# A new order of the calls on four engines in one period of a software-pipelined attention kernel

## The chip, the core and the metric

The kernel runs on 1 core of one Trainium2 chip. The metric is the device time of one execution in microseconds. Before the change three runs gave 4885.24 (median), 4884.3 and 4894.25 us.

## What is computed

A block of three parts on 8 x 256 tokens of width 256, in float32, each with a residual: half an FFN, an attention-like layer, half the same FFN. The layer has 16 heads. For each head it makes a query, four keys and four values a token by a projection, a causal convolution of width 4 and silu; the query and keys are normalised; a decay comes from a softplus of a low-rank projection. Then the state is carried over the tokens with a delta rule:

```python
M = tril(einsum(kg * exp(Gt - Gs), beta * kg), -1)        # chunk x 4 keys, square
u = solve_triangular(I + M, vg - einsum(kg * exp(G), S))
o = SCALE * (einsum(qg * exp(G), S) + einsum(attn, u))
S = exp(Glast)[..., None] * S + einsum(beta * kg * exp(Glast - G), u)
...
o = o * rsqrt(mean(o * o) + eps) * onorm_w * sigmoid(gate);  out = o @ Wo.T
```

## The kernel before

`build` cuts the 2048 tokens in NT = 4 tiles of 512 (two sequences), which with 16 heads makes NS = 64 sets. In a set there are 16 units of 32 tokens with 4 keys each, so that a unit is a matrix of 128 x 128; for each of the two sequences (hb = 0, 1) the eight units c = 0 to 7 follow one another through the state S.

The first FFN runs by itself. Then the sets run as a software pipeline: in period p (`for p in range(-1, NS + 3)`, L1045, L1430, L1805, L2010) every engine works on four sets, p to p - 3. Each engine has one list of calls written out by hand, one of the functions `delta_tensor` (L823), `delta_scalar` (L1168), `delta_vector` (L1541) and `delta_gpsimd` (L1940). An engine works through its list in order; between engines every call waits for counters that other calls raise (`nth`, `every`), so the order of a list decides what stands behind what, and never what is computed. Set p + 1 and p: `project_k`, `conv_k` (three taps on DVE after `tap_k` on ACT), `silu_k`, `decay`, `softplus`, `add_up` (a prefix sum), `factors` (exponentials). Set p - 1: `project_v`, `conv_v`, `silu_v`, `products` (for each quarter q of the set five levels l, whose scaled operands X come from `levels` on DVE and `level` on GpSimd), `evacuate` (Pd) and `keep` (E, At) of the results, `take`, `norm` (three small steps, the second after `length(0)` of ACT), `weigh`. Set p - 2: `begin` and `rows` on GpSimd, which invert the diagonal 32 x 32 blocks in 62 steps; when the last is done `unfold` and `turn` on DVE lay the result out, ACT's `place` (four copies) and `shift` put it in Ztf and Zc, and `first` to `fourth`, on PE and ACT by turns, build the inverse of the unit from it. Sets p - 2 and p - 3: the chunk steps `rhs`, `solve` and `update` of both sequences: PE `rhs`, DVE `rhs` (Rs), PE `solve`, ACT `solve` (Us), PE `update`, DVE `update` (S). At the end of set p - 3: ACT `out_square`, PE `mean_square`, ACT `out_root`, DVE `gated`, PE and DVE `output`.

The PSUM results (k, v, decay, norm, turned kdec and V, mean square, output, gate) share two banks in turn. `turns` (L692) takes a list in the order in which PE issues them (`bank_use`, L702) and gives every use its bank and the counter that says that the use before it on this bank is emptied; `acc_use` (L712) does so for three accumulators of the convolutions.

ACT's functions need one of two tables, with exp and ln or with silu and tanh. `e.preload_act_table_set` (L1444, L1471, L1510) names a point where the first is loaded ahead of its use; other switches are put in ahead of the function that needs them (they show under the helper line L1182).

In the last periods `spare(s, j)` calls (all four lists have them at points of the same name) do pieces of the second FFN (`DRAIN`, L23): a piece of gate and up matmuls, or of the down matmul. In all other periods they are empty.

## Time and profile before

| | |
|---|---|
| runs | 4885.24 us median (4884.3 to 4894.25) |
| span of the profiled execution | 4882.9 us |
| its own time beside the span | not given apart; the median of the runs is 2.3 us above the span |
| mean granted clock of TensorE | 0.979 |
| first FFN | the first 243 us or so |
| periods that follow one another in full | about 500 to 4510 us |
| last two periods and second FFN | 4510 us to the end |

The page gives the busy time of each engine as a share of the span; matmuls overlap, so a busy PE is not one at its peak. The trace behind it gives each instruction with its start, its length, and, where the engine stood idle before it, how long and which engine's work ended the wait. Two things matter in reading: a helper line stands for many calls (L835 for most matmuls, L1553 and L1556 for most of DVE, L1181 and L1182 for ACT), so operations are told by their tiles; and an instruction of DVE or ACT is longer than the distance to the next, because the two overlap.

### The profile page before, as it was taken

To read this page: it belongs to the slowest core of one execution; us is meant where nothing else is said; L and a number is where in the kernel's file an instruction comes from. 1 tells how busy PE (TensorE), PEld (TensorE's weight loads), DVE (VectorE), ACT (ScalarE), POOL (GpSimd) and SP (SyncE) were. 2 spreads that over 40 slices of the span, in tenths; PEclk is the share of its full clock that TensorE was granted. 3 is DMA by queue.
4 is the path that set the end of the run, shared out by engine and by line. 5 is a ranking of instruction groups with operands and counts; after the bars stand their busy time and mean duration, and the time that the engine had idled before them with its cause. 6 is when DMAs were issued, how large, how long until landed. Compare 5 with 4: busy or idle time off the path is not lost.

```text
span 4882.9 us, 151877 instructions
## 1 busy us (share of the span) xinstructions
PE 4493.2 (92%) x63200; PEld 3127.3 (64%) x63200; DVE 4052.7 (83%) x7262; ACT 3391.0 (69%) x6708; POOL 3362.7 (69%) x5828
## 2 busy tenths in 40 slices
...
GB/s 88 88 29 25 26 26 26 15 25 26 34 32 16 28 26 26 26 14 26 35 32 28 15 26 26 26 25 14 30 30 26 26 14 26 26 26 9 37 9 22
DMA packets 49727, 135.48 MB, mean 28 GB/s; under 512 B 7056, under 2 KB 28176, under 8 KB 48400
## 3 DMA queue, kind: packets, MB, share of 16 engines
...
## 4 chain that ended last, share of the span: by engine, by line
PE 58%; DVE 26%; ACT 9%; issue 6%; POOL 1%; DMA 0%; DVEq 0%; SPq 0%; ACTq 0%
PE bank L835 49%; DVE acc L1556 9%; PE bank L302 7%; DVE X L1553 6%; PE bank L906 2%; DVE Rs L1556 2%; DVE Pd L1661 2%; ACT o L1182 1%; DVE sp_t L1553 1%; DVE Zc L1740 1%; ACT Us L1181 1%; DVE o L1556 1%; ACT acc L1181 1%; ACT L1471 1%; ACT Ztf L1181 1%
## 5 line engine op out<-in xcount | busy, mean ns | idle before, releaser
L1556 DVE SCALAR_TENSOR_TENSOR acc<-bank,vc,acc 128x510 f32<-128x510 f32 (+2 forms) x1728 | 1270.9, 739 | 145.5 <-ACT acc L1181 120.0
L2006 POOL TENSOR_TENSOR LZ<-LZ,LT 128x120 f32<-128x120 f32 (+26 forms) x1984 | 979.5, 494 | 155.5
L2003 POOL TENSOR_TENSOR LT<-LA,LZ 128x120 f32<-128x120 f32 (+26 forms) x1984 | 877.8, 442 | 145.8
L1553 DVE TENSOR_TENSOR X<-KQ,Fl 128x640 f32<-128x640 f32 x1024 | 966.6, 960 | 0.9 <-ACT Fl L1182 0.9
L1976 POOL COPY X<-KQ 128x640 f32<-128x640 f32 x256 | 255.9, 1000 | 807.5 <-ACT F L1182 278.3
L835 PEld LDWEIGHTS bank<-X 128*32 128x32 f32 x32768 | 524.0, 112 | 301.0 <-issue 210.8
L1181 ACT ACTIVATE Us<-bank 128x128 f32<-128x128 f32 x1024 | 280.7, 277 | 627.8 <-PE bank L835 617.3
L835 PE MATMUL bank<-X 128*32 128x60 f32 (+1 forms) x32768 | 650.3, 205 | 64.4 <-issue 32.6
L835 PE MATMUL bank<-xnTm,WK 128*128 128x512 f32 x1280 | 660.8, 642 | 41.5 <-DVE acc L1556 35.8
L1951 POOL TENSOR_TENSOR kdec<-KQ,Fe 128x256 f32<-128x256 f32 x512 | 461.0, 921 | 152.3 <-PE bank L906 152.3
L835 PE MATMUL bank<-Rs,Ztf 128*128 128x128 f32 x2048 | 460.7, 312 | 68.1 <-DVE Rs L1556 48.0
L835 PE MATMUL bank<-xnTm,WV 128*128 128x512 f32 x1024 | 497.3, 608 | 12.8 <-ACT sg L1182 6.7
L1556 DVE SCALAR_TENSOR_TENSOR Rs<-V,knT,bank 128x128 f32<-128x128 f32 x896 | 308.1, 344 | 206.0 <-PE bank L835 194.2
L1181 ACT ACTIVATE acc<-bank,vc 128x512 f32<-128x512 f32 x576 | 393.7, 684 | 79.6 <-PE bank L835 77.2
L835 PEld LDWEIGHTS bank<-Rs,Ztf 128*128 128x128 f32 x2048 | 314.5, 191 | 193.5 <-DVE Rs L1556 113.9
L835 PE MATMUL bank<-Us,kdT 128*128 128x128 f32 x1792 | 399.5, 306 | 41.7 <-ACT Us L1181 23.6
L1951 POOL TENSOR_TENSOR kexp<-KQ,Fe 128x256 f32<-128x256 f32 x512 | 424.1, 855 | 0.0
L835 PEld LDWEIGHTS bank<-xnTm,WK 128*128 128x128 f32 x1280 | 230.2, 200 | 275.3 <-issue 172.1
L835 PE MATMUL bank<-S,kexp 128*128 128x128 f32 x1792 | 388.6, 299 | 3.2 <-ACT S L1181 2.6
L835 PE MATMUL bank<-qn,S 128*128 128x32 f32 x1792 | 349.2, 277 | 0.0
L835 PEld LDWEIGHTS bank<-S,kexp 128*128 128x128 f32 x1792 | 282.8, 192 | 80.1 <-issue 34.8
L835 PEld LDWEIGHTS bank<-Us,kdT 128*128 128x128 f32 x1792 | 272.6, 192 | 93.9 <-ACT Us L1181 78.7
...
## 6 DMA issues: line engine op xcount, KB each, us to landing
...
```

Source lines behind the costliest of these rows:

```text
L302: return e.matmul(o, l, r, start=start, stop=stop, skip_group_check=True)
L835: return e.matmul(o, l, r, start=start, stop=stop, skip_group_check=True)
L906: ins = e.transpose(o[:, P * c:P * c + P], kdec[:, c, :], ident)
L1181: return e.activation(o, i, f, scale=scale)
L1182: return e.activation(o, i, f, bias=bias, scale=scale)
L1553: return e.tensor_tensor(o, a, b, op)
L1556: return e.scalar_tensor_tensor(out=o, in0=a, scalar=sc, in1=b, op0=op0, op1=op1)
L1661: return e.copy_predicated(o, mk, d.rearrange("p n (a c) -> p n a c", c=c))
L1951: return e.tensor_tensor(o.rearrange("p u (g i t) -> p (u g) i t", g=4, i=R), kq[:, g0:g0 + 8, 0:R, :], f.unsqueeze(2).broadcast_to([P, 8, ...
L1976: e.tensor_copy(X0[:, :, 0:40], kk.rearrange("p g i t -> p g (i t)")).then_inc(g_copy, 1)
L2003: e.tensor_tensor(tmp, LA[:, j + 1:32, 8 * (j % R) + j // R].unsqueeze(2).broadcast_to([P, rr, cc]), LZ[:, j, 0:cc].unsqueeze(1).broadcast ...
L2006: e.tensor_tensor(LZ[:, j + 1:32, 0:cc], LZ[:, j + 1:32, 0:cc], tmp, SUB).then_inc(g_row, 1)
```

## The change

The four lists are laid out anew, and `bank_use` follows PE's new order (norm and the fourth turned V change places). No call is added or taken away, but the boundaries of a period are cut at other points, so that some calls stand in a period's head in one list and at the tail of the previous one in the other (`products(p, 0, 1)` for `products(p - 1, 0, 1)`, `length(p - 1, 1)` for `length(p - 2, 1)`). The first of the three `preload_act_table_set` calls now stands at the head of ACT's period. The diff, with the indentation taken off:

```diff
@@ -705,8 +705,8 @@
-("vturn", 2, 2, a_vt, 4, 2), ("turn", 0, 1, a_kdT, 4, 0), ("norm", 0, 0, v_max, 1, 0),
-("vturn", 3, 2, a_vt, 4, 3), ("turn", 1, 1, a_kdT, 4, 1), ("k", 0, -1, v_ck, 15, 2),
+("vturn", 2, 2, a_vt, 4, 2), ("turn", 0, 1, a_kdT, 4, 0), ("vturn", 3, 2, a_vt, 4, 3),
+("norm", 0, 0, v_max, 1, 0), ("turn", 1, 1, a_kdT, 4, 1), ("k", 0, -1, v_ck, 15, 2),
 ("k", 1, -1, v_ck, 15, 5), ("turn", 2, 1, a_kdT, 4, 2),
...
@@ -1043,59 +1043,58 @@
 for p in range(-1, NS + 3):
-rhs(p - 3, 0, 3)
-products(p - 1, 0, 1)
+update(p - 3, 1, 2)
+spare(p - 3, 7)
 solve(p - 3, 0, 3)
-update(p - 3, 1, 2)
-spare(p - 3, 8)
 turn(p - 2, 3)
 update(p - 3, 0, 3)
+spare(p - 3, 8)
 rhs(p - 3, 1, 3)
+rhs(p - 3, 0, 4)
 project_k(p, 2)
-rhs(p - 3, 0, 4)
 solve(p - 3, 1, 3)
+solve(p - 3, 0, 4)
+products(p - 1, 0, 2)
+update(p - 3, 1, 3)
...
 update(p - 3, 1, 5)
-spare(p - 3, 17)
-products(p - 1, 0, 4)
 solve(p - 3, 0, 6)
 rhs(p - 3, 1, 6)
+products(p - 1, 0, 4)
+spare(p - 3, 17)
 solve(p - 3, 1, 6)
-spare(p - 3, 19)
 update(p - 3, 0, 6)
 update(p - 3, 1, 6)
+spare(p - 3, 19)
+rhs(p - 3, 0, 7)
+rhs(p - 3, 1, 7)
+project_v(p - 1, 1)
 spare(p - 3, 20)
-rhs(p - 3, 0, 7)
-project_v(p - 1, 1)
 solve(p - 3, 0, 7)
-rhs(p - 3, 1, 7)
+solve(p - 3, 1, 7)
 project_k(p, 3)
-solve(p - 3, 1, 7)
+update(p - 3, 0, 7)
 spare(p - 3, 22)
-update(p - 3, 0, 7)
 update(p - 3, 1, 7)
+mean_square(p - 3)
 spare(p - 3, 23)
-mean_square(p - 3)
 project_k(p, 4)
...
@@ -1107,63 +1106,64 @@
 gate(p - 1)
 project_v(p - 1, 2)
+project_v(p - 1, 3)
 products(p - 1, 2, 0)
 products(p - 1, 2, 1)
-project_v(p - 1, 3)
+spare(p - 2, 30)
 first(p - 2, 0)
-spare(p - 2, 30)
 products(p - 1, 2, 2)
+spare(p - 2, 31)
 second(p - 2, 0)
-spare(p - 2, 31)
 products(p - 1, 2, 3)
+products(p - 1, 2, 4)
 turn_v(p - 2, 1)
-products(p - 1, 2, 4)
 third(p - 2, 0)
 spare(p - 2, 32)
 turn_v(p - 2, 2)
 turn(p - 1, 0)
 fourth(p - 2, 0)
 spare(p - 2, 33)
+turn_v(p - 2, 3)
 total(p)
-turn_v(p - 2, 3)
+first(p - 2, 1)
 products(p - 1, 3, 0)
-first(p - 2, 1)
-spare(p - 2, 34)
 products(p - 1, 3, 1)
-turn(p - 1, 1)
-second(p - 2, 1)
-spare(p - 2, 35)
 products(p - 1, 3, 2)
 products(p - 1, 3, 3)
+spare(p - 2, 34)
+second(p - 2, 1)
+products(p - 1, 3, 4)
+spare(p - 2, 35)
+turn(p - 1, 1)
 solve(p - 2, 0, 0)
-products(p - 1, 3, 4)
 project_k(p + 1, 0)
+update(p - 2, 0, 0)
 third(p - 2, 1)
+rhs(p - 2, 0, 1)
+fourth(p - 2, 1)
 spare(p - 2, 36)
-update(p - 2, 0, 0)
 project_k(p + 1, 1)
-fourth(p - 2, 1)
+solve(p - 2, 1, 0)
+solve(p - 2, 0, 1)
 spare(p - 2, 37)
-rhs(p - 2, 0, 1)
-solve(p - 2, 1, 0)
+update(p - 2, 1, 0)
+update(p - 2, 0, 1)
 spare(p - 2, 1)
-solve(p - 2, 0, 1)
-update(p - 2, 1, 0)
+rhs(p - 2, 1, 1)
 spare(p - 2, 2)
-update(p - 2, 0, 1)
-rhs(p - 2, 1, 1)
+rhs(p - 2, 0, 2)
 turn(p - 1, 2)
-rhs(p - 2, 0, 2)
 solve(p - 2, 1, 1)
+products(p, 0, 0)
+solve(p - 2, 0, 2)
+update(p - 2, 1, 1)
 spare(p - 2, 4)
-update(p - 2, 1, 1)
+products(p, 0, 1)
 spare(p - 2, 5)
-solve(p - 2, 0, 2)
 rhs(p - 2, 1, 2)
 update(p - 2, 0, 2)
-products(p, 0, 0)
 solve(p - 2, 1, 2)
-spare(p - 2, 7)
+rhs(p - 2, 0, 3)
...
@@ -1428,115 +1428,115 @@
 for p in range(-1, NS + 3):
-solve(p - 3, 1, 2)
-factors(p - 1, 3)
+e.preload_act_table_set("natural_log_exp_and_others")
 spare(p - 3, 7)
 solve(p - 3, 0, 3)
-turned(p - 2, 2)
+spare(p - 3, 8)
 silu_k(p, 0)
-silu_k(p, 1)
+turned(p - 2, 3)
+solve(p - 3, 1, 3)
+solve(p - 3, 0, 4)
 tap_k(p, 2)
-spare(p - 3, 8)
-solve(p - 3, 1, 3)
-turned(p - 2, 3)
 spare(p - 3, 10)
-solve(p - 3, 0, 4)
-e.preload_act_table_set("natural_log_exp_and_others")
-length(p - 2, 1)
+spare(p - 3, 11)
 factors(p - 1, 4)
-spare(p - 3, 11)
...
-decay(p, 1)
+spare(p - 3, 19)
+silu_k(p, 1)
+spare(p - 3, 20)
+tap_v(p - 1, 1)
+solve(p - 3, 0, 7)
+solve(p - 3, 1, 7)
 silu_k(p, 2)
-tap_v(p - 1, 1)
-spare(p - 3, 19)
-spare(p - 3, 20)
-solve(p - 3, 0, 7)
 silu_v(p - 1, 0)
-solve(p - 3, 1, 7)
 tap_k(p, 3)
+spare(p - 3, 22)
 out_square(p - 3)
 e.preload_act_table_set("natural_log_exp_and_others")
-decay(p, 2)
-spare(p - 3, 22)
 spare(p - 3, 23)
 out_root(p - 3, 0)
 out_root(p - 3, 1)
+decay(p, 1)
 keep(p - 1, 0)
 tap_k(p, 4)
 keep(p - 1, 1)
+decay(p, 2)
 silu_k(p, 3)
+gate_out(p - 1)
+shift(p - 2)
+turned_v(p - 2, 0)
 silu_v(p - 1, 1)
-gate_out(p - 1)
-turned_v(p - 2, 0)
-shift(p - 2)
 place(p - 2, 0)
+tap_v(p - 1, 2)
 place(p - 2, 1)
 place(p - 2, 2)
 place(p - 2, 3)
-tap_v(p - 1, 2)
+spare(p - 2, 30)
 silu_k(p, 4)
 tap_v(p - 1, 3)
+spare(p - 2, 31)
 first(p - 2, 0)
 square(p)
-spare(p - 2, 30)
 second(p - 2, 0)
-spare(p - 2, 31)
+keep(p - 1, 2)
 turned_v(p - 2, 1)
 third(p - 2, 0)
 spare(p - 2, 32)
 turned_v(p - 2, 2)
 turned(p - 1, 0)
+spare(p - 2, 33)
 fourth(p - 2, 0)
-keep(p - 1, 2)
-spare(p - 2, 33)
+silu_v(p - 1, 2)
+silu_v(p - 1, 3)
 turned_v(p - 2, 3)
-silu_v(p - 1, 2)
+rhs(p - 2, 0, 0)
 first(p - 2, 1)
-rhs(p - 2, 0, 0)
-silu_v(p - 1, 3)
 e.preload_act_table_set("natural_log_exp_and_others")
+spare(p - 2, 34)
+rhs(p - 2, 1, 0)
+spare(p - 2, 35)
 root(p, 0)
-spare(p - 2, 34)
-turned(p - 1, 1)
+solve(p - 2, 0, 0)
 second(p - 2, 1)
 root(p, 1)
-spare(p - 2, 35)
-solve(p - 2, 0, 0)
-rhs(p - 2, 1, 0)
 tap_k(p + 1, 0)
+update(p - 2, 0, 0)
+turned(p - 1, 1)
 third(p - 2, 1)
 factors(p, 0)
+spare(p - 2, 36)
 length(p - 1, 0)
-spare(p - 2, 36)
-update(p - 2, 0, 0)
 keep(p - 1, 3)
 fourth(p - 2, 1)
+factors(p, 1)
+solve(p - 2, 1, 0)
 spare(p - 2, 37)
-solve(p - 2, 1, 0)
+solve(p - 2, 0, 1)
+length(p - 1, 1)
+tap_k(p + 1, 1)
+update(p - 2, 1, 0)
+factors(p, 2)
 spare(p - 2, 1)
-solve(p - 2, 0, 1)
-update(p - 2, 1, 0)
-factors(p, 1)
-tap_k(p + 1, 1)
 spare(p - 2, 2)
 solve(p - 2, 1, 1)
-factors(p, 2)
+turned(p - 1, 2)
+factors(p, 3)
 spare(p - 2, 4)
+solve(p - 2, 0, 2)
 spare(p - 2, 5)
-solve(p - 2, 0, 2)
+solve(p - 2, 1, 2)
...
@@ -1803,139 +1803,139 @@
 for p in range(-1, NS + 3):
+spare(p - 3, 5)
+rhs(p - 3, 1, 2)
+update(p - 3, 0, 2)
 conv_k(p, 1, 1)
-spare(p - 3, 7)
 rhs(p - 3, 0, 3)
 conv_k(p, 1, 0)
+spare(p - 3, 7)
 levels(p - 1, 0, 2)
 update(p - 3, 1, 2)
+update(p - 3, 0, 3)
+spare(p - 3, 8)
 distance(p - 1, 4)
...
+spare(p - 3, 22)
 conv_k(p, 3, 2)
 conv_k(p, 3, 1)
-evacuate(p - 1, 0, 1)
+spare(p - 3, 23)
 conv_k(p, 3, 0)
-evacuate(p - 1, 0, 2)
 evacuate(p - 1, 0, 3)
 query(p - 1)
-spare(p - 3, 22)
-spare(p - 3, 23)
+lengths(p - 2)
 gated(p - 3, 0)
 gated(p - 3, 1)
 conv_k(p, 4, 2)
 conv_k(p, 4, 1)
+evacuate(p - 1, 1, 0)
 conv_k(p, 4, 0)
-evacuate(p - 1, 1, 0)
-output(p - 3, 0)
 evacuate(p - 1, 1, 1)
 evacuate(p - 1, 1, 2)
+output(p - 3, 0)
+evacuate(p - 1, 1, 3)
 output(p - 3, 1)
-evacuate(p - 1, 1, 3)
 unfold(p - 2, 0)
 unfold(p - 2, 1)
+levels(p - 1, 2, 1)
 turn(p - 2)
-levels(p - 1, 2, 1)
+softplus(p)
 levels(p - 1, 2, 2)
 levels(p - 1, 2, 3)
 levels(p - 1, 2, 4)
 conv_v(p - 1, 2, 2)
+spare(p - 2, 30)
 conv_v(p - 1, 2, 1)
+spare(p - 2, 31)
 conv_v(p - 1, 2, 0)
 conv_v(p - 1, 3, 2)
 conv_v(p - 1, 3, 1)
+evacuate(p - 1, 2, 0)
 conv_v(p - 1, 3, 0)
-evacuate(p - 1, 2, 0)
+levels(p - 1, 3, 1)
+spare(p - 2, 32)
+add_up(p)
 evacuate(p - 1, 2, 1)
+spare(p - 2, 33)
 evacuate(p - 1, 2, 2)
-levels(p - 1, 3, 1)
-softplus(p)
 levels(p - 1, 3, 2)
 evacuate(p - 1, 2, 3)
+levels(p - 1, 3, 3)
+levels(p - 1, 3, 4)
+spare(p - 2, 34)
 clamp(p)
-lengths(p - 2)
-levels(p - 1, 3, 3)
-add_up(p)
-levels(p - 1, 3, 4)
-distance(p, 1)
+spare(p - 2, 35)
 evacuate(p - 1, 3, 0)
 evacuate(p - 1, 3, 1)
 evacuate(p - 1, 3, 2)
+distance(p, 1)
 evacuate(p - 1, 3, 3)
 take(p - 1)
 scale(p)
+spare(p - 2, 36)
 norm(p - 1, 0)
 distance(p, 2)
+rhs(p - 2, 0, 1)
+norm(p - 1, 1)
 conv_k(p + 1, 0, 2)
-norm(p - 1, 1)
+norm(p - 1, 2)
 conv_k(p + 1, 0, 1)
-norm(p - 1, 2)
-spare(p - 2, 30)
-spare(p - 2, 31)
-spare(p - 2, 32)
-spare(p - 2, 33)
-spare(p - 2, 34)
-spare(p - 2, 35)
-spare(p - 2, 36)
 spare(p - 2, 37)
-rhs(p - 2, 0, 1)
 weigh(p - 1)
 conv_k(p + 1, 0, 0)
 spare(p - 2, 1)
+update(p - 2, 0, 1)
 spare(p - 2, 2)
-update(p - 2, 0, 1)
 rhs(p - 2, 1, 1)
 distance(p, 3)
 rhs(p - 2, 0, 2)
+conv_k(p + 1, 1, 2)
 levels(p, 0, 1)
 spare(p - 2, 4)
 update(p - 2, 1, 1)
-conv_k(p + 1, 1, 2)
-spare(p - 2, 5)
-rhs(p - 2, 1, 2)
-update(p - 2, 0, 2)
...
@@ -2023,11 +2023,11 @@
 spread(p - 1, 0, 0)
 spread(p - 1, 0, 1)
+spread(p - 1, 1, 0)
 spread(p - 1, 1, 1)
-spread(p - 1, 1, 0)
 spread(p - 1, 2, 1)
+spread(p - 1, 3, 1)
 spread(p - 1, 2, 0)
-spread(p - 1, 3, 1)
 level(p, 0)
```

## Rows read from the trace of the kernel before

**Rows 1.** The page, part 1: busy us, share of the span, instructions, by engine.
```profile
PE 4493.2 (92%) x63200; PEld 3127.3 (64%) x63200; DVE 4052.7 (83%) x7262; ACT 3391.0 (69%) x6708; POOL 3362.7 (69%) x5828
```
**Rows 2.** Windows view of four stretches: length, busy us by engine, clock, DMA share, GB/s.
```profile
436.39:4440.10 4003.71, 3745.78 (x57113) 2646.93 (x57112) 3620.05 (x6431) 3001.44 (x6019) 3105.64 (x5369) 0.99 0.07 25
2399.62:2468.30 68.68, 64.46 (x969) 45.11 (x969) 61.45 (x110) 50.85 (x102) 53.71 (x93) 0.98 0.10 35
3619.58:3686.45 66.87, 62.82 (x969) 44.62 (x969) 61.20 (x110) 50.82 (x103) 52.53 (x92) 1.00 0.09 31
...
2460.70:2464.20 3.50, 3.42 (x8) 1.05 (x12) 2.55 (x6) 2.16 (x5) 2.99 (x7) 0.57 0.00 0
```
**Rows 3.** Timeline of DVE, first and last of 60 turns: start us, length us.
```profile
436.39 0.71 DVE L1748 STREAM_TRANSPOSE Ztc<-Zc 128x512 f32<-128x512 f32 x1
...
4440.10 0.71 DVE L1748 STREAM_TRANSPOSE Ztc<-Zc 128x512 f32<-128x512 f32 x1
```
**Rows 4.** Timeline of PE, one period from its gate, and one wait in the tail.
```profile
3619.58 1.02 PE L835 MATMUL bank<-fgm,WV 128*128 128x512 f32 x2
...
3626.05 0.69 PE L835 MATMUL bank<-Zc,E 32*32 32x32 f32 x32
...
3627.28 0.21 PE L835 MATMUL bank<-Ys,Ztf 32*32 32x32 f32 x1 [0.15 <-ACT Ys L1181]
...
3634.66 0.52 PE L835 MATMUL bank<-X 128*32 128x60 f32 x24 [0.35 <-DVE Pd L1661]
...
3646.64 0.71 PE L835 MATMUL bank<-Rs,Ztf 128*128 128x128 f32 x4 [0.26 <-ACT Ztf L1181]
...
3670.58 0.49 PE L835 MATMUL bank<-Rs,Ztf 128*128 128x128 f32 x2 [0.44 <-DVE Rs L1556]
...
3678.51 1.10 PE L835 MATMUL bank<-o,cs 128*128 128x512 f32 x2 [0.78 <-ACT o L1182]
3680.05 1.98 PE L835 MATMUL bank<-xnTm,WK 128*128 128x512 f32 x4 [0.44 <-DVE acc L1556]
...
4691.71 1.06 PE L835 MATMUL bank<-Zc,E 32*32 32x32 f32 x32 [4.62 <-ACT Ztf L1181]
```
**Rows 5.** Timeline of ACT, opening of this period: place (four) and tap_v(2).
```profile
3622.55 2.59 ACT L1181 ACTIVATE Ztf<-Ztc 32x512 f32<-32x512 f32 x4
3625.17 0.69 ACT L1181 ACTIVATE acc<-bank,vc 128x512 f32<-128x512 f32 x1
```
**Rows 6.** Timeline of ACT, end of this period: out_square, decay(2), out_root(0).
```profile
3677.77 0.60 ACT L1182 ACTIVATE o<-bank 128x512 f32<-128x512 f32 x1
...
3679.68 0.72 ACT L1182 ACTIVATE rn<-rn,cs 128x512 f32<-128x512 f32 x1
3680.31 0.67 ACT L1182 ACTIVATE o<-bank,cs 128x512 f32<-128x512 f32 x1
```
**Rows 7.** Timeline of DVE, this period: norm(2), conv_k(4), the next unfold.
```profile
3646.05 0.25 DVE L1553 TENSOR_TENSOR Cn<-Cn,LB 128x32 f32<-128x32 f32 x1
...
3683.13 2.30 DVE L1556 SCALAR_TENSOR_TENSOR acc<-bank,vc,acc 128x510 f32<-128x510 f32 x3
...
3687.45 1.18 DVE L1740 STREAM_TRANSPOSE Zc<-LZ 128x256 f32<-128x256 f32 x2
```
**Rows 8.** Timeline of POOL, this period: begin and the last step of rows.
```profile
3646.36 0.53 POOL L1985 MEMSET LZ<- 128x512 f32 x1
...
3685.89 0.22 POOL L2006 TENSOR_TENSOR LZ<-LZ,LT 128x16 f32<-128x16 f32 x1
```
**Rows 9.** Timeline of ACT: a load in this period; two loads in the tail.
```profile
3655.72 1.28 ACT L1182 ACT_TABLE_LOAD   x1
3657.02 1.15 ACT L1182 ACTIVATE KQ<-acc 128x512 f32<-128x512 f32 x2
...
4793.80 1.28 ACT L1471 ACT_TABLE_LOAD   x1
...
4796.52 1.28 ACT L1510 ACT_TABLE_LOAD   x1
```

More of the change, by code:

```diff
@@ L1056, in delta_tensor @@
                 solve(p - 3, 1, 3)
+                solve(p - 3, 0, 4)
+                products(p - 1, 0, 2)
+                update(p - 3, 1, 3)
                 spare(p - 3, 10)
-                solve(p - 3, 0, 4)
-                update(p - 3, 1, 3)
+                rhs(p - 3, 1, 4)
+                update(p - 3, 0, 4)
                 spare(p - 3, 11)
-                update(p - 3, 0, 4)
-                rhs(p - 3, 1, 4)
                 project_v(p - 1, 0)
-                products(p - 1, 0, 2)
```

55 lines of the change are left out of this document (27 added, 28 removed).

## The prediction

> **What bounds it now.** The page's engine shares come first: TensorE (PE) 92% busy, VectorE (DVE) 83%, ScalarE (ACT) 69% [rows 1]. No engine is full, so order can matter. Next the stages: the stretch in which all sets overlap, 4003.71 us, is 59 periods between the first and the last turn of DVE [rows 2, 3], so 67.86 us for one. The period from 3619.58 takes 66.87 at full granted clock, the one from 2399.62 takes 68.68 with 3.5 us at 0.57 in it [rows 2]: an undisturbed period is 66.87, and about 1.0 of the mean is disturbance, partly the clock. I work on the undisturbed one, and count its times from its gate matmul (3619.58 is 0). Inside it the timeline of PE shows short waits [rows 4]: 0.15 for ACT's Ys, 0.35 for DVE's last Pd, 0.26 for ACT's Ztf, 0.44 for DVE's Rs in the chunk steps, then 0.78 for ACT's square and 0.44 for DVE's conv_k(3,0), which frees the bank of project_k(4). Adding small ones it is some 4 us in 66.87; an order can only win some of these. The path changes engine every few us, so I walked the new lists by hand: each operation begins when its engine has issued what stands ahead of it and its producer is done, with durations and start-to-start distances of the same operations in the old period. A wait on a short operation costs little, so distances matter: an isolated conv tap is 0.74 long, but the next begins 0.66 after it.
>
> **Opening: costs 0.63.** The four place copies take 2.59 on ACT and stand at 2.97 to 5.56 [rows 5]. In the new list decay(2) (0.65) stands ahead of the load and silu_k(3), silu_v(1) (0.6) stands behind turned_v(0), and tap_v(2) (0.69, [rows 5]) inside the four. The gate waits 0.27 longer, since evacuate(1,0) goes ahead of the last tap of conv_k(4) on DVE. By these the first place starts at 3.98 and the last ends at 7.19 in place of 5.56. PE reaches first(0) at 6.74 and stands 0.50 there (it began at 6.47 before, [rows 4]); with tap_v(3) and the Ys copy (ending 8.65) behind it, second(0) starts at 8.69, not 7.70, +0.99. Then cover comes back. conv_v(3,0) ends 0.8 later (softplus is ahead of it), in time for turn_v(2). add_up (1.2) goes ahead of evacuate(2,3), but PE no longer stands at products(3,0) for it: it does turn_v(3), total and first(1) first, so the 0.35 [rows 4] goes. PE has products(3,0) still to issue at 16.33; before it had issued it and first(1) at 16.26. That is 0.63 late with the 0.56 of products(3,0) counted.
>
> **Middle: gives back 0.46.** With turn(1) behind products(3,4) the wait of 0.20 for levels(3,4) goes, and project_k(0) ends at 22.07 against 21.81. third(1) on ACT now has tap_k(0), update(0,0) and turned(1) ahead of it (0.58 + 0.18 + 0.6), so PE waits 0.6 at fourth(1); project_k(1) behind it covers the wait of solve(1,0) for Ztf (0.26, [rows 4]). update(1,0) starts at 28.37 against 27.92; update(1,2), after conv_k(1,0..2) and levels(0,1) at DVE, at 35.00 against 35.16, with solve(0,3) (0.32) still to do: 0.17 late.
>
> **Chunk steps: win 0.56.** Each step is solve to update 0.86, update to S 0.51, S to rhs about 0.4, rhs to Rs 0.5, Rs to solve 0.4, and twelve of them must be threaded between the big matmuls. From 35 to 49 the two orders come out alike (update(1,5) begins 0.15 late). Then products(0,4) stands between rhs(1,6) and solve(1,6) and covers the wait of 0.44 for Rs [rows 4]; rhs(1,7) is ahead of project_v(1), and both solves ahead of project_k(3), whose 1.7 covers the Us copies. project_k(3) ends at 56.60 with solve(1,7) issued, against 56.99: 0.39 early.
>
> **End: wins 0.46 more.** silu_v(0) no longer holds ACT up at the end (Rs(1,7) is done early), so tap_k(3) starts at 56.7 instead of 57.37. out_square goes to 57.65 (58.19 before), and the mean-square matmul to 58.35 (58.93). decay(2) stood between the load and out_root(0) (60.10, 0.72) and held it to 60.73 [rows 6]; now decay(1) and decay(2) come after out_root(1), which gets gated to 60.95 (62.15 before). tap_k(4) begins at 61.95, behind project_k(4) and keep(0), and conv_k(4,2) at 62.70 where it began at 63.55 [rows 7], my mark for the period's end. 0.63 - 0.46 - 0.56 - 0.46 is -0.85: 66.02 for the period.
>
> **GpSimd sets a floor.** Its chain (begin at 26.78, rows, last row ending at 66.53: 39.75, [rows 8]) releases unfold, which started at 67.87, 1.34 later [rows 7]. From unfold at 1.01 to begin it is 25.77. So no period is below 25.77 + 39.75 = 65.52, plus what begin comes later after unfold. It waits for norm(2), at 26.47 [rows 7], and this for length(0), which ACT does behind third(1) and factors(0): 25.75 against 25.01. norm(2) starts at 26.97, 0.50 later: floor 66.02, as near to the walk as it can be. Two limits that meet cost a little more than either, so I take 0.7 of the 0.85, with bounds of 0.85 and 0.3.
>
> **One table load more: taken as nothing.** A load is 1.28, and the next activation starts 1.30 after its start [rows 9]. Old and new lists both switch three times to the set with exp and ln and three times back, but the load named at the head of the new period finds its set in place, and the old kernel's tail shows that such a load is executed: L1471 at 4793.80, two activations of that set, L1510 at 4796.52 [rows 9]. So seven loads instead of six, +1.30 on ACT. It lies between the copies of Us(1,2) and Us(0,3), at 35.0 to 36.3, and lets the second start 0.17 late; that is in the walk. Uncovered it would be 1.30. The Trainium skill ("ScalarE: Activation LUTs", What ACT_TABLE_LOAD costs) gives 1283 ns and a drain of about 1380 more for a switch. The trace agrees with the first and shows no room for the second. By the page the term would be up to 1.4 a period, and the sum would end above 4885; rival 3 is its case.
>
> **Other parts.** The swap of norm and vturn(3) in the bank rotation follows PE's order, and no bank is late in the walk by it (total needs turned(0), done at 13.85, and starts at 14.75). The GpSimd list swaps spread calls: kexp of all four quarters ends before the third kdec, near 19.5, and rhs(0,1) needs it at 23.6. DMA issues are unchanged. In the last two periods the FFN pieces move: spare 30 goes ahead of first(0), which had stood 4.62 for the place copies [rows 4]; the wait gets covered, between 0 and -4.6, I take -4.
>
> **Sum.** 62 full periods x -0.7 = -43.4, tail -4: -47. The profiled execution's span is 4882.9; the three runs are at 4884.3 to 4894.25, the median 4885.24, 2.3 above the span. 4885 - 47 = 4838.
>
> **Rivals.**
> (1) Slower: begin on GpSimd gets late. Its place is norm(1) on DVE, waiting for length(0) in ACT's queue. Every wait of PE before third(1) moves third, factors(0), length(0), norm(2) and begin as a whole. The floor passes 66.87 when norm(2) is over 1.35 later than before; I have 0.50, from a walk whose opening has 0.99 in it at one place. At 2.0 late the floor is 67.52, +0.65 a period: 4885 + 40 = 4925. For: durations with their full length instead of distances give a norm(2) later than 1.0. Against: PE's 1.34 on unfold was slack [rows 7, 8].
> (2) No net change: norm(2) 1.35 late, or the PE waits that go come back two operations on: 4885.
> (3) Slower: the load at the head of the period holds ACT for twice its row (2 x 1.28), because something must run dry behind the Us copy ahead of it. Us(0,3) then starts at 37.6, update(0,3) at 37.93 instead of 36.64; if nothing of these 1.3 is won back the period is 66.17 + 1.3 = 67.47, and the time 4885 + 37 - 4 = 4918. Against it: 1.30 from start to start [rows 9]. For it speaks only the drain that the Trainium skill ("ScalarE: Activation LUTs", What ACT_TABLE_LOAD costs) puts behind a load.
> (4) More than forecast: the stretch that had the clock at 0.57 [rows 2] is where PE waited for square and conv_k(3,0) [rows 4]; with those waits shorter the clock falls in fewer periods. Half of the 1.0 of disturbance would go, 0.5 x 62 = 31 more: 4807.
> (5) The lists do not hold the same work: then busy time and counts of DVE or PE differ in the new page. I read the same calls in both, but for that load.
>
> **Numbers.** Forecast 0.50 (4838, own range 4815 to 4868), rival 4 0.12, rivals 2 and 5 0.10, rival 1 0.23, rival 3 0.05. Within 0.2% is 10 us, about what a measurement of this kernel can tell from no change. Faster 0.62, same 0.10, slower 0.28. The range takes in rival 4 with the full 0.85 (4885 - 53 - 4 - 31 = 4797, and 12 below it, as the share of disturbance that goes is a guess) and rival 1 up to 4930; 2 in 10 are left out at both ends together.
>
> **What would show it.** Right: undisturbed periods of 66.0 to 66.4; PE standing about 0.5 at first(0) and 0.4 at second(0); no wait at products(3,0), none at solve(1,6); out_root(0) directly after the mean-square matmul; unfold close behind GpSimd's last row; 7 loads a period. Wrong: undisturbed periods at or above 66.87, norm(2) over 1.3 later after unfold, PE waits for Us behind the first load, or more periods with the lower clock.

## The result, and the profile after

The changed kernel takes 5051.7 us in the median of its runs (5033.48 to 5078.57), against 4888.56 for the kernel before on the same chip: a ratio of 1.033, 95% interval [1.029, 1.037]. Forecast was 4838 with a range up to 4930; it is slower, and outside the range. The profiled execution took 5061.88, its span is 5060.1.

The page of the kernel after, part 1 and the group of part 5 with the short matmuls of `products`; the last line is that group on the page of the kernel before, which has the same form (to the right of the bar: busy us, mean ns | idle just before them, and what ended most of it):

```profile
PE 4548.7 (90%) x63200; PEld 3235.3 (64%) x63200; DVE 3935.1 (78%) x7262; ACT 3461.6 (68%) x6770; POOL 3218.2 (64%) x5828
...
L835 PE MATMUL bank<-X 128*32 128x60 f32 (+1 forms) x32768 | 629.1, 206 | 87.5 <-issue 66.0
```
```profile
L835 PE MATMUL bank<-X 128*32 128x60 f32 (+1 forms) x32768 | 650.3, 205 | 64.4 <-issue 32.6
```

Counts are those of [rows 1], but for 62 more on ACT: the table loads at the head of a period. PE is busy 55 us longer with the same 63,200 matmuls, so some of them ran slower (the mean granted clock of the run is 0.952, against 0.979); and the part of its idle time that ends on "issue" (PE waited for nothing that the profile shows) doubled at the short matmuls.

The windows view of after answers to [rows 2]; its columns are the same. First 59 periods from gate matmul to gate matmul, then an undisturbed period, a disturbed one, and two stretches inside the disturbed one:

```profile
502.21:4675.06 4172.85, 3805.63 (x57113) 2759.27 (x57112) 3510.25 (x6432) 3068.46 (x6077) 2968.82 (x5367) 0.96 0.07 24
...
2060.74:2126.63 65.89, 61.75 (x970) 45.01 (x969) 59.65 (x110) 51.84 (x104) 49.90 (x89) 1.00 0.07 24
2334.34:2410.19 75.85, 66.78 (x969) 48.39 (x968) 58.95 (x110) 52.17 (x104) 51.56 (x95) 0.93 0.06 21
2343.50:2345.70 2.20, 0.11 (x3) 0.04 (x4) 0.49 (x1) 1.10 (x3) 1.27 (x2) 1.00 0.63 248
2346.80:2353.60 6.80, 6.80 (x47) 5.88 (x45) 5.66 (x10) 3.01 (x6) 1.78 (x2) 0.50 0.00 0
```

And 59 periods of before, taken in the same way:

```profile
502.51:4507.45 4004.94, 3747.42 (x57114) 2647.89 (x57114) 3620.42 (x6432) 3000.75 (x6018) 3104.95 (x5369) 0.99 0.07 25
```

An undisturbed period has become shorter, 65.89 against 66.87 [rows 2]. The mean period has become longer: 4172.85 / 59 = 70.73 against 67.88. So what disturbs a period costs 4.8 us in the mean, where it cost 1.0. In 59 periods that is 167.9 us; the stretch behind them grew by 9.6 (385.0 against 375.5), and the one ahead of them shrank by 0.3, which together is the difference of the spans, 177.2. In the fourth line PE does almost nothing for 2.2 us while the DMA engines are 63% busy; in the fifth it is busy all the time at a granted clock of 0.50.

The timeline of PE in this disturbed period (start, length, operation, in brackets the idle time before it), from its gate to 20 us behind it; the many rows of the 32-row matmuls of `second` are left out:

```profile
2334.34 1.12 PE L835 MATMUL bank<-fgm,WV 128*128 128x512 f32 x2
2335.30 0.60 PE L897 MATMUL bank<-cs,V 128*128 128x128 f32 x4
2336.24 3.70 PE L835 MATMUL bank<-xnTm,WV 128*128 128x512 f32 x8 [0.34 <-ACT sg L1182]
2339.87 0.91 PE L835 MATMUL bank<-X 128*32 128x60 f32 x64
...
2343.35 0.22 PE L835 MATMUL bank<-X 128*32 128x40 f32 x1
2345.66 1.24 PE L835 MATMUL bank<-X 128*32 128x40 f32 x31 [2.09 <-issue]
2346.83 1.12 PE L897 MATMUL bank<-cs,V 128*128 128x128 f32 x4
2347.87 1.97 PE L835 MATMUL bank<-Zc,E 64*64 64x64 f32 x16
```

Up to 9.01 us it is the undisturbed period. Then PE has issued one of the 32 matmuls of a block of `products` and stands 2.09, and no engine is named. Behind it every operation takes nearly double: `third` 1.97 where the undisturbed period has 1.14. PE reaches project_k(0) 8.2 us later than in the undisturbed period: 3.3 of that are two such waits (this one and one of 1.24 at 25.8 us), and the rest is about half of the 10.2 us at the lower clock.

The same view of the undisturbed period, its waits in the opening (all of 0.3 or more from the gate to 24 us), which answers to [rows 4]:

```profile
2062.65 3.70 PE L835 MATMUL bank<-xnTm,WV 128*128 128x512 f32 x8 [0.34 <-ACT sg L1182]
...
2067.62 0.69 PE L835 MATMUL bank<-Zc,E 32*32 32x32 f32 x32 [0.43 <-ACT Ztf L1181]
...
2069.13 0.21 PE L835 MATMUL bank<-Ys,Ztf 32*32 32x32 f32 x1 [0.43 <-ACT Ys L1181]
...
2084.59 1.14 PE L835 MATMUL bank<-Ztf,Y 64*64 64x64 f32 x16 [0.55 <-ACT Y L1181]
```

Added up over 59 periods from the timeline of PE (waits of 0.5 us and more that end on "issue"): before 31 of them, 26.6 us, 27 at 18 to 21 us of a period; after 80, 123.0 us, of which 36 at 9 to 15 us (69.4), 12 at 15 to 22 (13.8), 24 at 22 to 30 (26.1) and 8 behind 58 us (13.7). All the 24 at 22 to 30 us are in periods that had a wait at 9 to 15 us and are late by then. The 36 periods with a wait at 9 to 15 us take 73.01 in the mean, the 16 without any issue wait 66.73. The stretches at half the clock in the same 59 periods: before 75 us in 22, 20 of them near 60 us of a period; after 358 us in 51, all but two of them before 36 us of a period. Of these 51, 30 (287 us) begin within an issue wait or at most 6 us behind it, and each of the 18 longest waits (2.05 us and more) has one within or behind it; the other 21 are 3.4 us each, most of them near 25 and 33 us, and their cause stays open.

**What an "issue" wait is.** The DMA view of the stall above, two short windows, with the queues' packets, megabytes and share of the 16 engines:

```profile
q1 hardware_dynamic: 71, 0.32, 93.5%
```
```profile
q1 hardware_dynamic: 35, 0.16, 96.6%
q8 instruction: 1, 0.02, 17.5%
```

The first is 2342.0 to 2342.9, the second 2343.0 to 2343.4. Queue q8 moved 498 packets of 16 KB in the whole run, and PE executed 126,400 matmuls and weight loads and 1,191 others besides: 256 to a packet, so q8 is PE's instruction stream. A period of about 1,940 such instructions is 7.6 packets long, so where in the list a packet ends moves from period to period. Here the packet starts in the window 2343.0 to 2343.4, and PE goes on at 2345.66. I put the start of the q8 packet ahead of it beside every "issue" wait of 0.5 us or more: PE goes on 2.2 to 2.8 us behind the packet's start in all 31 of before (median 2.50), and 2.2 to 3.3 in 78 of the 80 of after (median 2.42). Such a wait is PE having executed all that it had been sent, and counting shows it: with PE's recorded instructions numbered in order of their start, the one that ends a wait has the number 256 x N + 193 to 195, where N is the number of q8 packets begun by then, in all 31 waits of before, all 80 of after and every one of the twelve runs below. Every wait is at the end of a packet. In before none of them begins ahead of its packet's start; in after nine do, by up to 0.95 us: there PE was dry before the next packet had even started.

### The profile page after: what moved, and what is told of

Read it like the earlier page. It is cut to its first block, busy times and chain, and to the rows that moved or that the text cites. A ratio compares the mean times of both kernels' runs of the same rounds, so it can differ in the third digit from the quotient of the medians.

```text
span 5060.1 us, 151938 instructions
## 1 busy us (share of the span) xinstructions
PE 4548.7 (90%) x63200; PEld 3235.3 (64%) x63200; DVE 3935.1 (78%) x7262; ACT 3461.6 (68%) x6770; POOL 3218.2 (64%) x5828
## 4 chain that ended last, share of the span: by engine, by line
PE 64%; ACT 17%; DVE 11%; issue 7%; POOL 1%; DMA 0%; SPq 0%; DVEq 0%; ACTq 0%
PE bank L835 51%; DVE acc L1556 7%; PE bank L302 7%; ACT Ztf L1181 3%; PE bank L897 3%; ACT acc L1181 3%; PE bank L906 3%; ACT Zc L1181 1%; ACT Us L1181 1%; ACT rn L1182 1%; ACT KQ L1182 1%; ACT V L1182 1%; ACT V L1181 1%; DVE S L1556 1%; ACT Y L1181 1%
## 5 line engine op out<-in xcount | busy, mean ns | idle before, releaser
L2006 POOL TENSOR_TENSOR LZ<-LZ,LT 128x120 f32<-128x120 f32 (+26 forms) x1984 | 952.5, 480 | 155.5
L2003 POOL TENSOR_TENSOR LT<-LA,LZ 128x120 f32<-128x120 f32 (+26 forms) x1984 | 906.3, 457 | 145.8
L1553 DVE TENSOR_TENSOR X<-KQ,Fl 128x640 f32<-128x640 f32 x1024 | 913.7, 907 | 1.4 <-ACT Fl L1182 1.4
L1976 POOL COPY X<-KQ 128x640 f32<-128x640 f32 x256 | 184.1, 719 | 861.5 <-PE bank L835 344.5
L1181 ACT ACTIVATE Us<-bank 128x128 f32<-128x128 f32 x1024 | 269.2, 276 | 648.2 <-PE bank L835 646.9
L835 PE MATMUL bank<-X 128*32 128x60 f32 (+1 forms) x32768 | 629.1, 206 | 87.5 <-issue 66.0
L1951 POOL TENSOR_TENSOR kdec<-KQ,Fe 128x256 f32<-128x256 f32 x512 | 436.9, 874 | 405.6 <-PE bank L906 405.6
L835 PE MATMUL bank<-Rs,Ztf 128*128 128x128 f32 x2048 | 411.3, 299 | 14.0 <-DVE Rs L1556 11.2
L1951 POOL TENSOR_TENSOR kexp<-KQ,Fe 128x256 f32<-128x256 f32 x512 | 395.6, 804 | 0.0
L1556 DVE SCALAR_TENSOR_TENSOR S<-S,egl,bank 128x128 f32<-128x128 f32 x768 | 258.5, 343 | 132.2 <-PE bank L835 126.0
```

What stands on the lines that cost most here:

```text
L835: return e.matmul(o, l, r, start=start, stop=stop, skip_group_check=True)
L1181: return e.activation(o, i, f, scale=scale)
L1553: return e.tensor_tensor(o, a, b, op)
L1556: return e.scalar_tensor_tensor(out=o, in0=a, scalar=sc, in1=b, op0=op0, op1=op1)
L1951: return e.tensor_tensor(o.rearrange("p u (g i t) -> p (u g) i t", g=4, i=R), kq[:, g0:g0 + 8, 0:R, :], f.unsqueeze(2).broadcast_to([P, 8, ...
L1976: e.tensor_copy(X0[:, :, 0:40], kk.rearrange("p g i t -> p g (i t)")).then_inc(g_copy, 1)
```

## The experiments

Theory F: an "issue" wait is a late instruction packet. Blocks of short matmuls use up 256 instructions faster than the next packet comes, the weight loads (WV, WK), released by project_v(3), delay the packet, and the clock falls behind the wait. Rival A: PE's waits for ACT at first(0) and second(0) let the clock fall. In after these waits are 0.43 us each in all 59 periods; of 0.2 us and more, before has a single one, of 0.41 at second(0). Others are the rivals of the prediction. The base kernels: `b_` is the kernel before, `a_` the kernel after, `bl_` is a_back_late below. In the table, the period is the mean of 59 in the profiled execution, "shortest" the shortest one of them, "issue" the sum of such waits of 0.5 us or more and "half clock" the time at the lower clock, both in the same 59 periods. The expectations below count half clock between 400 and 4550 us of the run, which takes in some of what follows the 59 periods: 102 for before, 352 for after, 102 for a_back_late.

| kernel | time, us | ratio to before, 95% interval | period | shortest | issue | half clock |
|---|---|---|---|---|---|---|
| before | 4888.56 | | 67.88 | 66.87 | 26.6 | 75 |
| after | 5051.70 | 1.033 [1.029, 1.037] | 70.73 | 65.74 | 123.0 | 358 |
| b_pv3_early | 5098.06 | 1.043 [1.040, 1.047] | 71.27 | 66.93 | 110.8 | 365 |
| a_pv3_back | 4924.17 | 1.008 [1.005, 1.010] | 68.26 | 65.72 | 74.2 | 137 |
| a_wk_first | 4992.91 | 1.021 [1.017, 1.024] | 69.49 | 65.72 | 85.9 | 273 |
| a_small_loads | 4891.67 | 1.001 [0.999, 1.002] | 67.62 | 65.70 | 58.4 | 79 |
| a_open_back | 4885.36 | 0.997 [0.996, 0.999] | 67.67 | 66.10 | 42.4 | 92 |
| a_late_loads | 4885.92 | 0.997 [0.996, 0.999] | 67.77 | 65.72 | 61.3 | 92 |
| b_late_loads | 4883.97 | 0.999 [0.997, 1.000] | 67.96 | 66.86 | 25.0 | 96 |
| a_back_late | 4840.54 | 0.989 [0.987, 0.990] | 66.86 | 66.09 | 23.2 | 31 |
| bl_split_out | 4906.74 | 1.004 [1.002, 1.006] | 67.97 | 67.27 | 14.0 | 44 |
| bl_no_head_load | 4835.53 | 0.989 [0.987, 0.990] | 66.93 | 66.02 | 26.5 | 44 |
| bl_tapv_only | 4838.01 | 0.989 [0.986, 0.991] | 66.86 | 65.91 | 20.4 | 44 |
| bl_act_open | 4812.59 | 0.984 [0.982, 0.986] | 66.55 | 65.43 | 22.1 | 48 |

**One call of PE put back in the new kernel (a_pv3_back):**

```
                 project_v(p - 1, 2)
-                project_v(p - 1, 3)
                 products(p - 1, 2, 0)
                 products(p - 1, 2, 1)
+                project_v(p - 1, 3)
```

> The kernel after, with one call of PE's list put back: project_v(3) behind products(2,1) again. Theory F (in the opening PE's sequencer runs out of instructions, the 'issue' waits of 1 to 3.7 us at 9.8 to 14 us of a period, and the clock falls behind them): if the block of short products directly ahead of first(0) is what empties it, the issue waits shrink from 80 (123 us) to under 50, and the time falls to 4900 to 4990. Theory A (PE's waits for ACT at first(0) and second(0), 0.4 each, let the clock fall): no change of those waits, time stays at 5030 to 5080.

**The reverse of that edit, in the kernel before (b_pv3_early): project_v(3) ahead of products(2,0).**

> The kernel before, with PE's project_v(3) moved ahead of products(2,0), as the change has it; ACT, DVE and all else as before. Theory F with this call as the cause (it starts the weight loads 1 us earlier and puts all short matmuls behind it): issue waits of 1 to 3 us appear at 9 to 14 us of many periods, half clock behind them, time 4950 to 5050. If the cause is ACT's later opening (theory A), or something else of the change: 4880 to 4910.

The one call, moved ahead of two blocks of `products` in the kernel before, makes it slower than the whole change did: +209 us, with the lists of ACT, DVE and GpSimd untouched; forecast was at most 5050. Moved back in the new kernel it returns 128 of 163 us. The issue waits of a_pv3_back are 56 (74.2 us), not under 50, and the time is within what was expected. These two runs alone do not put rival A out. In a_pv3_back the wait at first(0) is 0.23, where it was 0.43, with that at second(0) still 0.43; and b_pv3_early, whose ACT list is the old one, has a wait of 0.35 for ACT at second(0) in every period, which before had not. What puts it out is a_small_loads and a_late_loads below: both keep the two waits at 0.43 in all 59 periods, and the half clock falls from 358 to 79 and 92 us.

A disturbed period of b_pv3_early in the timeline of PE, from 5.4 us behind its gate (790.33), again without the rows of `second`, in which PE stands 2.85 on "issue", and two stretches of it in the windows view:

```profile
795.76 0.91 PE L835 MATMUL bank<-X 128*32 128x60 f32 x64
796.61 0.69 PE L835 MATMUL bank<-Zc,E 32*32 32x32 f32 x32
797.23 0.45 PE L835 MATMUL bank<-X 128*32 128x20 f32 x32
...
801.50 0.25 PE L835 MATMUL bank<-Ztf,Ys 32*32 32x32 f32 x1 [2.85 <-issue]
...
801.85 0.75 PE L835 MATMUL bank<-X 128*32 128x40 f32 x16
802.53 1.12 PE L897 MATMUL bank<-cs,V 128*128 128x128 f32 x4
```
```profile
798.20:801.90 3.70, 0.85 (x50) 0.67 (x43) 2.88 (x4) 0.28 (x1) 3.70 (x6) 0.69 0.65 252
801.90:813.30 11.40, 11.40 (x83) 8.75 (x82) 3.85 (x9) 4.62 (x10) 2.91 (x5) 0.50 0.01 3
```

64 + 32 + 32 short matmuls, with their weight loads 256 instructions, are issued from 795.76 to 797.68, in 1.9 us. Next to them a projection is eight instructions in 1.98 us. Where the project_v(3) between them is gone, PE runs dry; DMA is at 0.65 and 252 GB/s with the weights in that stretch, and the 11.4 us behind it run at half the clock.

**The weight loads made small (a_small_loads).** From the third set on they move 32 columns only, so the weights of later sets are wrong; all waits stay. The load of WK is changed in the same way.

```
-                e.dma_start(WV[:, s % 2, :], wv[s % H]).then_inc(d_wv[s % 2], 16)
+                if s < 2:
+                    e.dma_start(WV[:, s % 2, :], wv[s % H]).then_inc(d_wv[s % 2], 16)
+                else:
+                    e.dma_start(WV[:, s % 2, 0:32], wv[s % H][:, 0:32]).then_inc(d_wv[s % 2], 16)
```

> The kernel after; from the third set on, the loads of WV and WK move 32 columns in place of 2816 and 2304 or so, so the weights of the later sets are wrong and the 1.25 MB a period are not moved; all waits stay. Theory F with the weight transfers as its cause (the instruction fetch of PE stands behind them in the DMA engines): the issue waits in the opening go (under 20 us in all), the stretches at half clock in the opening with them, and the time is 62 x 66.0 to 66.5 plus the rest, 4830 to 4870. If fetches run dry by the density of PE's instructions alone: issue waits stay above 80 us and the time above 4980. Theory A: unchanged, 5030 to 5080.

Neither as strong nor as weak as expected. Without the traffic the waits at 9 to 15 us shrink from 36 with 69.4 us to 12 with 8.1, and 160 us go. But the waits at 15 to 30 us stay, 33 with 39.2 us where after has 36 with 39.9: there PE's list alone (first(1) and four blocks of products(3,*) in a row) empties the stream. No issue wait of this kernel begins ahead of its packet's start.

**WK's load ahead of WV's in SP's list (a_wk_first)**, as it may be issued after project_k(4):

> The kernel after with SP's list changed alone: the load of WK, whose buffer is free after project_k(4), is issued ahead of that of WV, so some 0.7 of the 1.25 MB move 7 us earlier, beside project_k(4) and products(1,*), and the burst behind project_v(3) is half as long. Theory F with the transfers as its cause: fewer issue waits at 9.8 to 14 us (half of their 80 us), time 4880 to 4980, though they can come at 2 to 6 us instead. Instruction density alone, or theory A: 5030 to 5080.

4993, outside the 4880 to 4980 expected: half the burst at the bad place helps by 59 us only, but in the direction: the issue waits at 9 to 15 us are 34.9 where they were 69.4.

**PE's second stretch put back too (a_open_back):**

```
                 total(p)
+                products(p - 1, 3, 0)
                 first(p - 2, 1)
-                products(p - 1, 3, 0)
+                spare(p - 2, 34)
                 products(p - 1, 3, 1)
+                turn(p - 1, 1)
+                second(p - 2, 1)
+                spare(p - 2, 35)
                 products(p - 1, 3, 2)
                 products(p - 1, 3, 3)
-                spare(p - 2, 34)
-                second(p - 2, 1)
-                products(p - 1, 3, 4)
-                spare(p - 2, 35)
-                turn(p - 1, 1)
                 solve(p - 2, 0, 0)
+                products(p - 1, 3, 4)
```

> The kernel after with two stretches of PE's list put back: project_v(3) behind products(2,1), and products(3,0..4) taken apart by first(1), turn(1), second(1) and solve as before; everything else, ACT, DVE and GpSimd too, as after. Theory F (blocks of short matmuls packed together use up PE's 256 fetched instructions faster than the next fetch, 3 us, brings more): the issue waits at 15 to 22 us fall from 40 us in 33 (a_pv3_back) to about 22 us in 27, as before the change, and the time to 4840 to 4870, under the kernel before, since undisturbed periods stay near 66. If PE's order in these places is not what makes them: 4915 to 4935 as a_pv3_back.

The waits at 15 to 22 us fell from the 40.0 of a_pv3_back to 13.7, but the time to 4885 only, 15 above what I gave: 15.6 us of issue waits at 9 to 15 us remain and 12.6 at 60 to 80, and so do 92 us at half clock. The shortest period is 66.10, not 65.72: putting this stretch back costs 0.4.

**The weight loads late (a_late_loads, b_late_loads), and with PE's two stretches put back (a_back_late).** The loads wait for project_k(1) as well, near 26 us of a period:

```
             def load_wk(s):
                 w.wait_ge(p_decay, every(s - 2, 1))
-                w.wait_ge(p_k, every(s - 2, 5))
+                w.wait_ge(p_k, every(s - 2, 5) + (2 if s >= 2 else 0))
...
                 w.wait_ge(p_v, every(s - 2, 4))
+                if s >= 2:
+                    w.wait_ge(p_k, every(s - 1, 5) + 2)
```

> The kernel after with the loads of WV and WK held on SP until project_k(1) is done, near 26 us of the period in place of 6; PE's, ACT's and DVE's lists are those of after. Theory F with the transfers lengthening a fetch: the long issue waits (1 to 3.7 us) at 9 to 15 us shrink as in a_small_loads to 12 short ones, those at 15 to 22 stay, and the time is 4880 to 4920; issue waits may come at 28 to 36 us, where PE has few short matmuls, so few. If the density of short matmuls alone sets them: 5000 and up.

> The kernel before with the weight loads late alone. Theory F: before, the opening has no issue waits at 9 to 15 us, those at 19 us come behind the end of the transfers; so little changes, 4870 to 4890. If the transfers make the waits at 19 us too: 4850 to 4870.

> Both: PE's two stretches as before and the weight loads late. Theory F: the fewest issue waits of all, under 25 us, time 4820 to 4860. If the two edits repair the same thing: the better of the two alone, 4840 to 4870.

All three as theory F has them. The late loads take 166 us out of the new kernel with every other engine's list as it is, all the bytes moved, and nothing in return at their new place: no issue wait at 30 to 60 us. To the kernel before they do almost nothing. Together with PE's two stretches the new kernel is at 4840.5, 1.1% under the one before, with 23.2 us of issue waits. The time lies in both of its expected ranges; that it is 45 us under either edit alone, and has the fewest issue waits of the runs so far, speaks for theory F.

Its mean and one undisturbed period in the windows view:

```profile
502.07:4446.53 3944.46, 3698.96 (x57113) 2662.18 (x57112) 3541.25 (x6432) 3064.79 (x6078) 3046.58 (x5366) 1.00 0.07 25
2168.64:2234.77 66.13, 62.31 (x970) 44.98 (x969) 60.15 (x110) 51.95 (x104) 51.84 (x91) 1.00 0.07 24
```

The mean is 0.7 above the undisturbed one; in the kernel before it was 1.0, in the kernel after 4.8. The half clock near 60 us of a period, 20 stretches in before, is down to 8, though the waits for ACT's square (0.78) and for conv_k (0.49) there have not become shorter; why is open.

**The block of products(1,*) broken up (bl_split_out):** output(0) between products(1,2) and products(1,3).

> a_back_late (PE's two stretches as before, weight loads late) with one call more moved: output(0) between products(1,2) and products(1,3), so that the run of 320 instructions of products(1,*) is broken by four long matmuls. Theory F: the issue waits at 60 to 80 us of a period (7, 12.2 us in a_back_late) fall to under 3 us, and with the half clock behind them the time falls by 8 to 25, to 4815 to 4833. If such a block has nothing to do with them: 4838 to 4843, or a little more, since products(1,3) comes later to DVE.

Theory F was right for the issue waits at 60 to 80 us, which fell from 12.2 to 2.4, and wrong for the rest: the half clock did not fall with them (31 us in the 59 periods, now 44), and the time rose by 66. The timeline of PE in three periods running:

```profile
2002.70 1.13 PE L837 MATMUL bank<-WO,o 128*128 128x256 f32 x4 [1.08 <-DVE acc L1558]
...
2069.99 1.13 PE L837 MATMUL bank<-WO,o 128*128 128x256 f32 x4 [1.08 <-DVE acc L1558]
...
2137.97 1.13 PE L837 MATMUL bank<-WO,o 128*128 128x256 f32 x4 [1.08 <-DVE acc L1558]
```

output(0) takes a bank that the last tap of conv_k on DVE frees, and the blocks of `products` had covered that. Now PE stands 1.08 in all 59 periods (63.9 us in sum); 62 x 1.08 = 67 is about the loss.

**Without the load at the head of ACT's list (bl_no_head_load):**

> a_back_late without the table load at the head of ACT's list, which finds its set in place. My prediction's walk: it delays Us(0,3) by 0.17 us a period, so 0 to -10 us, 4830 to 4843. Rival 3 (the load holds ACT for 2.6 us and this is on the path): -1.3 x 62 = -80, 4760.

4835.5 against 4840.5, the same ratio to before: the seventh load costs nothing that can be measured, and rival 3 is out.

**ACT's opening put back (bl_act_open), and half of it (bl_tapv_only, on bl_no_head_load):**

```
+                silu_v(p - 1, 1)
                 gate_out(p - 1)
-                shift(p - 2)
                 turned_v(p - 2, 0)
-                silu_v(p - 1, 1)
+                shift(p - 2)
                 place(p - 2, 0)
-                tap_v(p - 1, 2)
                 place(p - 2, 1)
                 place(p - 2, 2)
                 place(p - 2, 3)
+                tap_v(p - 1, 2)
```

> a_back_late with ACT's opening as before the change: silu_v(1) ahead of gate_out, tap_v(2) behind the four place copies. My walk: PE's wait of 0.4 at first(0) goes (the copies end 0.7 to 1.2 earlier), and second(0) starts earlier; if the period keeps it, -0.4 x 62 = -25, 4815; if another wait takes its place, 4835 to 4845. Theory A (these waits are what lets the clock fall) would have the half-clock time fall from 102 us to under 50 as well.

> bl_no_head_load with one call of ACT moved: tap_v(2) behind the four place copies, silu_v(1) left behind turned_v(0) and gate_out first, so that PE's project_v(2) gets its bank from the gate as early as in a_back_late. If bl_act_open gains by the earlier end of the place copies and pays 0.5 us a period at project_v(2), this keeps most of the first without the second: 4795 to 4815. If what counted there was silu_v(1) (the copy V that turn_v and the DVE evacuations want): 4830 to 4843.

bl_act_open is the fastest of all, 4812.6, 1.6% under before and near the 4815 expected; its shortest period is 65.43. By the count of the expectation its half-clock time is 96 us, not under 50, and in the 59 periods it is 48 against the 31 of a_back_late, though both waits are gone: these waits did not set the clock here either. bl_tapv_only, at 4838, misses the 4795 to 4815 of its first expectation and falls in the second range, whose reason (the copy V) was not tested. What became of the gain is in the opening. In the timeline of PE, undisturbed periods: first a_back_late, then bl_tapv_only, then bl_act_open.

```profile
2175.54 0.69 PE L837 MATMUL bank<-Zc,E 32*32 32x32 f32 x32 [0.25 <-ACT Ztf L1183]
...
2177.04 0.21 PE L837 MATMUL bank<-Ys,Ztf 32*32 32x32 f32 x1 [0.43 <-ACT Ys L1183]
```
```profile
2176.84 0.69 PE L837 MATMUL bank<-Zc,E 32*32 32x32 f32 x32
...
2178.67 0.21 PE L837 MATMUL bank<-Ys,Ztf 32*32 32x32 f32 x1 [0.76 <-ACT Ys L1183]
```
```profile
2311.24 1.98 PE L837 MATMUL bank<-xnTm,WV 128*128 128x512 f32 x4 [0.60 <-ACT sg L1184]
...
2315.91 0.69 PE L837 MATMUL bank<-Zc,E 32*32 32x32 f32 x32
```

With tap_v(2) behind the copies the wait at first(0) goes, and the one at second(0) grows by 0.33: ACT still has tap_v(2), silu_k(4) and tap_v(3) ahead of the Ys copy. With silu_v(1) gone too from between gate_out and the copies, both go, for 0.60 at project_v(2) in place of 0.34.

## Why the prediction was wrong

**Opening costs 0.63, middle gives back 0.46, chunk steps win 0.56, end wins 0.46: the sum and the waits right, the sizes of the first three not.** The sum was a period of 66.02; undisturbed ones of after take 65.74 to 66.1. Point by point in the one from 2060.74: the first place copy starts at 3.69 (3.98 forecast), the last ends at 6.83 (7.19), PE stands 0.43 at first(0) (0.50) and 0.43 at second(0) (0.4), nothing at products(3,0) or solve(1,6), 0.55 at fourth(1) (0.6); the mean-square matmul starts at 57.94 (58.35). But PE has issued first(1) at 15.80 with 0.56 of products(3,0) to come, so the opening cost 0.10, not 0.63. project_k(0) ends, by the start of the next matmul, at 21.11 (22.07), update(1,2) starts at 34.33 (35.00), project_k(3) ends at 56.18 (56.60) and conv_k(4,2) starts at 62.27 (62.70): the middle gave 0.61, the chunk steps 0.30, the end 0.47. At its own mark the walk would have won 1.28, not 0.85, and the period won 0.98, because GpSimd's chain came up to it; that the sum of the terms lay near is in part luck. ACT's end of this period, which answers to [rows 6], then DVE's next unfold and POOL's begin and last step of rows, which answer to [rows 7, 8]:

```profile
2117.93 0.60 ACT L1182 ACTIVATE o<-bank 128x512 f32<-128x512 f32 x1
2118.55 1.28 ACT L1467 ACT_TABLE_LOAD   x1
2119.84 0.69 ACT L1182 ACTIVATE o<-bank,cs 128x512 f32<-128x512 f32 x1
```
```profile
2061.39 1.16 DVE L1740 STREAM_TRANSPOSE Zc<-LZ 128x256 f32<-128x256 f32 x2
...
2127.28 1.16 DVE L1740 STREAM_TRANSPOSE Zc<-LZ 128x256 f32<-128x256 f32 x2
```
```profile
2087.57 0.52 POOL L1985 MEMSET LZ<- 128x512 f32 x1
...
2126.93 0.22 POOL L2006 TENSOR_TENSOR LZ<-LZ,LT 128x16 f32<-128x16 f32 x1
```

out_root(0) starts as the load ends, with no decay(2) between. From unfold to begin it is 26.18 us (25.77 before, so 0.41 later, where I had 0.50), from begin to the last row's end 39.58, and the next unfold starts 0.13 behind it: 65.89 in all. The new order does run into GpSimd's floor, at the place forecast and within 0.15 of the size. Rival 1 did not come: no lateness of 1.35 in an undisturbed period.

**One table load more, taken as nothing: right.** ACT_TABLE_LOAD at the head of the list is executed, 34.3 us into this period, which makes seven a period, and bl_no_head_load puts its price at nothing that can be measured.

```profile
2095.04 1.28 ACT L1431 ACT_TABLE_LOAD   x1
```

The rule of 2.66 us for a switch (the Trainium skill, "ScalarE: Activation LUTs", What ACT_TABLE_LOAD costs) shows in no row here: in the rows of ACT's end above, the next activation starts 1.29 behind the load's start.

**Tail, -4: wrong, and small.** The wait of 4.62 for the place copies is 1.72 in the new kernel (the row below), but the stretch behind the last gate counted above is 9.6 us longer. Its issue waits (5.9 us) and half clock (71) are about those of before (6.4 and 79), so they do not explain it; in a_back_late this stretch is longer still, 391 against the 375.5 of before. The cause stays open.

```profile
4860.93 0.69 PE L835 MATMUL bank<-Zc,E 32*32 32x32 f32 x32 [1.72 <-ACT Ztf L1181]
```

**The step that failed** is the one by which the sum was made: "an undisturbed period is 66.87, and about 1.0 of the mean is disturbance", and then 62 times the gain of the undisturbed period, with the disturbance carried over as it was, or halved (rival 4). It came out at 4.8 instead: (4.8 - 1.0) x 62 = 236 us lost, -1.0 x 62 = -60 won, +176 in all, and the profiled executions differ by 177. The list of things that would show me wrong has "more periods with the lower clock", but no rival had it as its mechanism, and none was priced near 5050. The rows that I read held the clue: PE waits that end on "issue" are in the trace of before (31 of them) and on its page, 32.6 us at the short matmuls, and the prediction counts no instructions. The Trainium skill ("Runtime: NRT & Kernel Launch", Instruction fetch mechanics) describes the fetch in blocks of 16 KB or 256 instructions while the current block executes, and says that the cost of crossing a boundary is "mostly hidden". The trace agrees with the block's size (498 packets of 16 KB for 127,591 instructions). It does not agree that the crossing is hidden: 123 us of waits, and the clock behind them.

How the loss is made, then: (1) project_v(3), 1.9 us of eight instructions, stood behind two blocks of `products` and ahead of first(0), and was moved ahead of all three; first(1) and products(3,0..3) were joined likewise. PE then asks for 256 instructions in under 2 us, and goes on only 2.4 to 2.5 behind the start of a packet. (2) project_v(3) releases the weight loads, 1.28 MB at about 250 GB/s, which are in the DMA engines at that very time; a packet then starts late, and a wait at 9 to 15 us, 0.6 to 0.7 in the mean of the runs without the loads there, becomes 1.9 in the mean and up to 3.7. (3) Behind the longest of these the granted clock is 0.5, and the opening, a chain of small matmuls between ACT copies, takes 8 us more in the disturbed period shown. No run takes the clock's share apart from that of the waits. An estimate from the rows: over the 59 periods the issue waits are 96 us more than before, the half clock 358 - 75 = 283 us more, and if half of that is lost, 142; the two make 238, where the disturbance grew by 226.

Left open: why the packet is asked for so late (the trace shows when it starts, not what asked for it), what lowers the clock in the 21 short stretches that follow no issue wait, what makes the tail longer, and whether another length of period in instructions (7.6 packets now) would do better. None of these was tried.
